# A vision tower on one core: the load queue waits for the token weights after tile 0's loads, the weights come in three parts, and one constant product goes

## The chip, the core and the metric

The kernel runs on one core of a Trainium2 chip. A core has TensorE (PE in the profile; PEld is its weight load), VectorE (DVE), ScalarE (ACT), GpSimd (POOL) and SyncE (SP), which here issues all DMAs. Each engine works through its own instructions in their order and waits on semaphores for the others. The metric is the device time of one launch in microseconds, as the median of several runs.

## The reference

The input is 32 images of 3 x 96 x 96 in fp32. Each is cut into 36 patches of 16 x 16 x 3 = 768 values, 1152 tokens in all. A token layer, an attention layer over channels and a layer of soft experts follow. The part that the change touches is the first:

```python
p = x.reshape(B, C, h, PATCH, w, PATCH).transpose(0, 2, 4, 3, 5, 1)
p = p.reshape(B, h * w, PATCH * PATCH * C)
p = _layernorm(p, ln1_g, ln1_b)               # over the 768 values
y = jnp.einsum('bnd,de->bne', p, W_proj)      # 768 -> 192
return _layernorm(y, ln2_g, ln2_b)
```

After it, h = layernorm(h + attention(h)), where queries, keys and values are products of h with 192 x 576 weights, and h = layernorm(h + experts(h)) with 8 experts of 4 slots each. All of it is fp32.

## The kernel before

The 1152 tokens are nine tiles of 128 for the token layer, and eleven groups of three images (108 tokens) for the rest. The first norm isn't applied to x. Its gain, its mean and its offset are folded into the weights: TensorE sums the weights' columns with the gain over 768 (`column_means`, L459, six products of 128 x 192, into `csp`), VectorE makes `wc = wt * gain - csp` in six pieces (`token_weights`, L713), TensorE makes the offset row (`offset`, L468, six products), and VectorE copies it (`token_offset`, L718). Then `token(t)` multiplies the turned tile xT with wc (L480, six products), and `token_out` (L740) scales the result by 1 / sigma of the token, which comes from the statistics of the plain tile xs (`x_stats`, L726, on VectorE; the power on GpSimd, L1211). So every tile is loaded twice, turned (`load_turned`, L375) and plain (`load_x`, L380), 384 KB each. The second norm follows, and `turn_h` (L491) turns h for the QKV products (L506 to L515).

An fp32 product is one MATMUL in the code and two passes, two entries, in the trace.

All engines' orders are written out by hand as lists of calls (L435 for the load queue, L680 for TensorE, L983 for VectorE). On TensorE the list starts with `first_products`: six products of a constant tile `still`, whose result nobody reads, right after VectorE has set that tile. Then come the column means, the offset, `token(0)`, `token(1)`, `token(2)`, and `turn_h(0)`.

SyncE's list starts with the first norm's gain and offset (gb), the token weights wt in two parts of three 128-row chunks each (288 KB a part, semaphores `wtok_in[0]` and `wtok_in[1]`), and tile 0's two loads. The identity, tile 1's two loads, tile 2's turned load, the small loads of the second norm, tile 3's turned load, tile 2's plain one, the three QKV weights and further tiles follow. The plain tiles have four buffers, so from tile 4 on `load_x(t)` waits until the statistics of tile t - 4 are done. The column means wait for the part of wt that holds their chunk, the offset for all parts.

Of the kernel before, what the change touches and what calls it, by code (L numbers as in the profile page):

```python
# [32 lines left out]
D = 192  # L33
HEADS, DH = 8, D // 8
PD = CH * PATCH * PATCH
KC = PD // 128
GI = 3
NG = (B + GI - 1) // GI
NT = NTOK // 128
# [7 lines left out]
NEG = -1.0e30  # L47
NQN = 2 * GI
NN = NQN + 2 * GI * DH
EPS_TOK, EPS_LN, EPS_L2 = 1e-6, 1e-5, 1e-6  # L50


def images(g):
    return min(GI, B - g * GI)


def tokens(g):
    return images(g) * TOK


def pieces(g):

    a, e, out = g * GI * TOK, g * GI * TOK + tokens(g), []
    while a < e:
        n = min(e, (a // 128 + 1) * 128) - a
        out.append((a // 128, a % 128, a - g * GI * TOK, n))
        a += n
    return out


def last_tile(g):
    return pieces(g)[-1][0]


def build(nc, x, x_t, w_tok, ln1_gb, ln2_g, ln2_b, g2col, b2col, w_qk, w_v, w_rest, w_proj, b_proj, temp, slots, scale,
# [3 lines left out]
    with ctx:  # L79
        def sb(name, shape):  # L80
            return ctx.enter_context(nc.sbuf_tensor(name, shape, F32))

        def sem(name):
            return ctx.enter_context(nc.semaphore(name))
# [4 lines left out]
        negmask = sb("negmask", [128, GI * SL])  # L89
        gb1 = sb("gb1", [128, 2, KC])  # L90
        gs1 = sb("gs1", [128, KC])
        wt = sb("wt", [128, KC, D])
        wc = sb("wc", [128, KC, D])
        bw = sb("bw", [128, D])
# [33 lines left out]
        y1 = sb("y1", [128, NB, D])  # L128
        xT = sb("xT", [128, KC * NTOK])
        st2 = sb("st2", [128, 2, 6])  # L130
# [60 lines left out]
        def csp():  # L191
            return ps[:, 0, 0:D]

        def bwp():
            return ps[:, 1, 0:D]
# [61 lines left out]
        h0_in = [sem(f"h0_in{g}") for g in range(NG)]  # L257
        ident_in = sem("ident_in")
        ln1_in = sem("ln1_in")
        wtok_in = [sem(f"wtok_in{i}") for i in range(2)]  # L260
        ln2_in = sem("ln2_in")
        wqkv_in = sem("wqkv_in")
        rows_in = sem("rows_in")
# [99 lines left out]
        @block.sync  # L363
        def _(sp):
            def load_norm1():
                sp.dma_start(gb1[:, :, :].rearrange("p t k -> p (t k)"), ln1_gb).then_inc(ln1_in, 16)

            def load_token_weights(i):
                k0 = i * KC // 2
                sp.dma_start(wt[:, k0:k0 + KC // 2, :].rearrange("p k e -> p (k e)"),  # L370
                             w_tok[:, k0 * D:(k0 + KC // 2) * D]).then_inc(wtok_in[i], 16)

            def load_turned(t):
                o = t * 128 * KC
                sp.dma_start(xT[:, o:o + KC * 128], x_t[:, o:o + KC * 128]).then_inc(xT_in[t], 16)  # L375

            def load_x(t):
                if t >= NB:
                    sp.wait_ge(st1_ready, t - NB + 1)
                sp.dma_start(xs[:, t % NB, :], x[t * 128:t * 128 + 128, :]).then_inc(x_in[t], 16)  # L380

            def load_ident():
                sp.dma_start(ident[:, :], ident_h).then_inc(ident_in, 16)

            def load_norm2():
                sp.dma_start(g2[:, :], g2col).then_inc(ln2_in, 16)
                sp.dma_start(b2[:, :], b2col).then_inc(ln2_in, 16)

            def load_imgsel():
                sp.dma_start(imgsel[:, :], imgsel_h).then_inc(imgsel_in, 16)  # L390

            def load_qkv():
                sp.dma_start(wqk[:, :], w_qk).then_inc(wqkv_in, 16)
                sp.dma_start(wv[:, :, :].rearrange("p m c -> p (m c)"), w_v).then_inc(wqkv_in, 16)
                sp.dma_start(wrest[:, :], w_rest).then_inc(wqkv_in, 16)

            def load_attention():
                sp.dma_start(tempc[:, :], temp).then_inc(attn_in, 16)
                sp.dma_start(wp[:, :, :], w_proj).then_inc(attn_in, 16)

            def load_rows():
                sp.dma_start(g2row[:, :], ln2_g.partition_broadcast(128)).then_inc(rows_in, 16)
                sp.dma_start(b2row[:, :], ln2_b.partition_broadcast(128)).then_inc(rows_in, 16)
                sp.dma_start(bprow[:, :], b_proj.partition_broadcast(128)).then_inc(rows_in, 16)

            def load_slots():
                sp.dma_start(negmask[:, :], negmask_h).then_inc(negmask_in, 16)
                sp.dma_start(spraw[:, :, :, :].rearrange("p f n q -> p f (n q)"),
                             slots.rearrange("(f p) n q -> p f (n q)", f=2)).then_inc(slots_in, 16)
                sp.dma_start(scl[:, :], scale.broadcast_to([F, 1])).then_inc(slots_in, 16)  # L410

            def load_experts():
                sp.dma_start(wd[:, :, :, :].rearrange("p f n h -> p f (n h)"), w_down).then_inc(experts_in, 16)
                sp.dma_start(bd[:, :], b_down).then_inc(experts_in, 16)
                sp.dma_start(own[:, :], own_h).then_inc(experts_in, 16)
                sp.dma_start(bu[:, :], b_up).then_inc(experts_in, 16)
                sp.wait_ge(cleared, 6)
                for j in range(4):
                    sp.dma_start(wu[32 * j:32 * j + HID, :, :], w_up[j]).then_inc(experts_in, 16)

            def regroup(g):
                sp.wait_ge(r_ready, last_tile(g) + 1)
                for t, p, q, n in pieces(g):
                    sp.dma_start(z[q:q + n, g, :], h0[p:p + n, t, 0:D]).then_inc(h0_in[g], 16)

            def store(g):
                if g < NG - 1:
                    sp.wait_ge(o4_ready, g + 1)
                else:
                    sp.wait_ge(o4_last, 1)  # L430
                ov = out.rearrange("b n d -> (b n) d")
                sp.dma_start(ov[g * GI * TOK:g * GI * TOK + tokens(g), :],
                             o4[0:tokens(g), g % NQ, :]).then_inc(out_done[g % NQ], 16)

            load_norm1(); load_token_weights(0); load_token_weights(1); load_turned(0); load_x(0)  # L435
            load_ident(); load_turned(1); load_x(1); load_turned(2); load_norm2(); load_turned(3)
            load_x(2); load_qkv(); load_turned(4); load_imgsel(); load_x(3); load_x(4); load_turned(5)
            load_turned(6); load_x(5); load_rows(); load_attention(); load_x(6); load_slots(); load_x(7)
            load_turned(7); load_x(8); load_turned(8); regroup(0); regroup(1); regroup(2); regroup(3)
            regroup(4); regroup(5); regroup(6); regroup(7); regroup(8); regroup(9); load_experts()  # L440
            regroup(10); store(0); store(1); store(2); store(3); store(4); store(5); store(6); store(7)
            store(8); store(9); store(10)
            for i in range(NQ):
                sp.wait_ge(out_done[i], 16 * len(range(i, NG, NQ)))

# [2 lines left out]
        def _(pe):  # L448
            def first_products():
                pe.wait_ge(still_ready, 1)  # L450
                for _ in range(6):
                    pe.matmul(ps[:, 2, 0:D], still[:, 0:128], still[:, :], start=True, stop=True)

            def column_means():
                pe.wait_ge(gs1_ready, 1)
                for kc in range(KC):
                    if kc % (KC // 2) == 0:
                        pe.wait_ge(wtok_in[kc // (KC // 2)], 16)
                    mm = pe.matmul(csp(), gs1[:, kc:kc + 1].broadcast_to([128, 128]), wt[:, kc, :],  # L459
                                   start=kc == 0, stop=kc == KC - 1)  # L460
                mm.then_inc(csp_ready, 1)

            def offset():
                pe.wait_ge(ln1_in, 16)
                pe.wait_ge(wtok_in[0], 16)
                pe.wait_ge(wtok_in[1], 16)
                for kc in range(KC):
                    mm = pe.matmul(bwp(), gb1[:, 1, kc:kc + 1].broadcast_to([128, 128]), wt[:, kc, :],  # L468
                                   start=kc == 0, stop=kc == KC - 1)
                mm.then_inc(bwp_ready, 1)  # L470
# [881 lines left out]
```

## Time and profile before

| | us |
|---|---|
| median of 3 runs | 112.63 (112.24 to 112.75) |
| the profiled execution | 112.18 |
| its span in the trace | 110.4 |
| TensorE busy with matmuls in the span | 101.7 |
| VectorE, ScalarE, GpSimd busy | 87.7, 67.5, 53.4 |

The span runs from the first instruction to the last. Times in the trace count from its start; what the profiled execution took beyond it lies before and after. A busy TensorE isn't TensorE at its peak, as matmuls are pipelined. A DMA's time "to landing" is counted from the start of its issue to the semaphore's last increment, and an issue of SyncE takes time itself.

### The profile page before, as it was taken

How to read it: one execution, taken by the hardware profiler on the slowest of the kernel's cores; microseconds unless marked ns; L12 is line 12 of the kernel's file. 1: busy time of each engine (PE TensorE's matmuls, PEld its weight loads, DVE VectorE, ACT ScalarE, POOL GpSimd, SP SyncE). 2: the span in 40 equal slices, each digit the busy share in tenths (PEclk: the TensorE clock that was granted, in tenths of full speed). 3: DMA queues.
4: the chain of work that ended last, by engine and by line, in shares of the span. 5: the costliest groups of instructions: out<-in, count | busy, mean ns of one | idle time of the engine just before them, and what ended most of it. 6: DMA issues, size and time to landing. Idle time of an engine off the chain costs nothing. (4 is left out here: it accounts for less than half of the span.)

```text
span 110.4 us, 4479 instructions
## 1 busy us (share of the span) xinstructions
PE 101.7 (92%) x1607; PEld 88.2 (80%) x1607; DVE 87.7 (79%) x380; ACT 67.5 (61%) x222; POOL 53.4 (48%) x126
## 2 busy tenths in 40 slices
PE   6999999999999999999999999799989989999900
PEld 6999989979999887887898887679779668879500
DVE  2129756968998958958977989999999897999960
ACT  4000023729563887798887996787785994476570
POOL 8800552263999887847204417906030340076880
PEclk9999999999999999999999999999999999999996
DMA  2999999469501111111000000010042000002232
GB/s 23 334 339 394 389 386 398 153 212 342 235 0 30 36 32 40 29 35 32 6 3 6 0 6 0 6 48 24 30 105 72 7 0 3 0 6 84 66 112 58
DMA packets 8554, 11.27 MB, mean 102 GB/s; under 512 B 2358, under 2 KB 5878, under 8 KB 8534
## 3 DMA queue, kind: packets, MB, share of 16 engines
q1 hardware_dynamic: 8533, 11.00, 29.5%
q8 instruction: 13, 0.21, 0.8%
q14 instruction: 8, 0.06, 0.2%
HBM read 9.22 MB, written 0.88 MB: 92 GB/s over the span
## 5 line engine op out<-in xcount | busy, mean ns | idle before, releaser
L480 PE MATMUL ps<-wc,xT 128*128 128x192 f32 x108 | 19.1, 330 | 0.0
L480 PEld LDWEIGHTS ps<-wc,xT 128*128 128x128 f32 x108 | 17.4, 190 | 0.7 <-issue 0.6
L1046 ACT ACTIVATE hT<-ps,b,g 128x128 f32<-128x128 f32 x18 | 7.3, 463 | 16.4 <-PE ps L491 16.3
L1068 ACT ACTIVATE km<-ps,imgsel 108x192 f32<-108x192 f32 (+1 forms) x32 | 11.1, 420 | 3.7 <-PE ps L515 3.6
L1256 POOL TENSOR_SCALAR mv<-mv 108x1 f32<-108x1 f32 (+1 forms) x11 | 3.0, 270 | 14.4 <-DVE mv L856 14.4
L568 PE MATMUL ps<-wp,yT 128*108 128x192 f32 (+1 forms) x44 | 9.3, 333 | 0.0
L664 PE MATMUL ps<-wu,hb 128*96 128x192 f32 (+1 forms) x44 | 9.2, 332 | 0.1
L1261 POOL TENSOR_TENSOR r<-mv,halves 108x2 f32<-108x2 f32 (+1 forms) x11 | 8.8, 803 | 0.8
L508 PE MATMUL ps<-wqk,hT 128*108 128x192 f32 (+1 forms) x44 | 9.0, 326 | 0.0
L726 DVE BATCH_NORM_STATS2 st<-xs 128x6 f32<-128x384 f32 x18 | 8.9, 537 | 0.0
L1249 POOL TENSOR_TENSOR rqt<-rn,tempc 128x6 f32<-128x6 f32 x11 | 2.2, 199 | 12.1 <-ACT rn L1105 12.1
L1207 POOL TENSOR_SCALAR var<-mv 128x1 f32<-128x1 f32 x9 | 2.0, 219 | 11.8 <-DVE mv L731 11.5
L1078 ACT ACTIVATE sqk<-km 108x576 f32<-108x576 f32 (+1 forms) x11 | 7.5, 683 | 0.0
L664 PEld LDWEIGHTS ps<-wu,hb 128*96 128x96 f32 (+1 forms) x44 | 6.5, 161 | 0.8 <-issue 0.4
L593 PE MATMUL ps<-sp,xnT 96*108 96x96 f32 (+1 forms) x44 | 6.2, 264 | 0.7 <-ACT xnT L1111 0.4
L568 PEld LDWEIGHTS ps<-wp,yT 128*108 128x108 f32 (+1 forms) x44 | 6.4, 170 | 0.5 <-DVE yT L836 0.2
L559 PE MATMUL ps<-vT,pc 32*32 32x37 f32 x512 | 6.8, 195 | 0.0
L1162 ACT ACTIVATE o<-z,sh,rstd 108x192 f32<-108x192 f32 x10 | 5.1, 543 | 2.8 <-DVE sh L980 2.8
L1269 POOL TENSOR_TENSOR rstd<-var,mhalf 108x1 f32<-108x1 f32 (+1 forms) x11 | 6.3, 576 | 0.9
L506 PE MATMUL ps<-hT,wv 128*128 128x108 f32 (+1 forms) x44 | 6.6, 273 | 0.0
L559 PEld LDWEIGHTS ps<-vT,pc 32*32 32x32 f32 x512 | 5.5, 104 | 1.3
L508 PEld LDWEIGHTS ps<-wqk,hT 128*108 128x108 f32 (+1 forms) x44 | 6.4, 171 | 0.0
(118 smaller groups left out, 296.6 us busy)
## 6 DMA issues: line engine op xcount, KB each, us to landing
xT<-in_x_t SPq DMA_DIRECT2D x9, 384.0 KB, 6.4
xs<-in_x SPq DMA_DIRECT2D x9, 384.0 KB, 6.2
out<-o SPq DMA_DIRECT2D x10, 81.0 KB
wt<-in_w_tok SPq DMA_DIRECT2D x2, 288.0 KB, 3.2
wqk<-in_w_qk SPq DMA_DIRECT2D x1, 192.0 KB, 5.9
wp<-in_w_proj SPq DMA_DIRECT2D x1, 192.0 KB, 10.0
wd<-in_w_down SPq DMA_DIRECT2D x1, 192.0 KB
z<-h SPq DMA_DIRECT2D x2, 81.0 KB
```

What stands on the lines that cost most here:

```text
L480: mm = pe.matmul(tokp(t), xT[:, o + kc * 128:o + (kc + 1) * 128], wc[:, kc, :], start=kc == 0, stop=kc == KC - 1)
L506: pe.matmul(vp(g)[:, m, :], wv[:, m, :], main, start=True, stop=False)
L508: pe.matmul(qkp(g)[:, m, :], main, wqk[:, m * D:(m + 1) * D], start=False, stop=False)
L559: mm = pe.matmul(yp(g)[r, m, i, :], pc[r, g % 2, GI * m + i, :], vT[r, m, g * GI + i, :], start=True, stop=True, tile_position=(32 * j, 32 ...
L568: mm = pe.matmul(prp(g), yT[:, g % NY, m, 0:images(g), :].rearrange("p i n -> p (i n)"), wp[:, m, :], start=m == 0, stop=m == 1)
L664: mm = pe.matmul(ytp(g), hb[:, e, i0:i0 + ni, :, :].rearrange("p i n q -> p (i n q)"), wu[:, e, :], start=e == 0, stop=e == 1)
L726: ins = dve.bn_stats(st1[:, t % 2, h, :], xs[:, t % NB, h * (PD // 2):(h + 1) * (PD // 2)])
L1046: ins = act.activation(hT[:, f, t * 128:(t + 1) * 128], htp(t)[:, f, :], ACT.Identity, bias=b2[:, f:f + 1], scale=g2[:, f:f + 1])
L1068: act.activation(km[0:n, g % NK, i, :], qkp(g)[:, 1, :], ACT.Copy, scale=imgsel[0:n, i:i + 1])
L1078: act.activation(sqk[0:n, g % 2, 0:ni, :], km[0:n, g % NK, 0:ni, :], ACT.Square).then_inc(sqk_ready, 1)
L1261: pool.tensor_tensor(r3[0:n, g, :], mv3[0:n, g, 1:3], halves[0:n, :], ALU.pow).then_inc(r3_ready, 1)
L1269: pool.tensor_tensor(rstd4[0:n, g:g + 1], var4[0:n, g:g + 1], mhalf[0:n, 0:1], ALU.pow).then_inc(rstd4_ready, 1)
```

## The change

The token weights come in three parts of two chunks, 192 KB each, with a semaphore for each. Behind the first tile's two loads SyncE waits until the last part has landed, and then issues the identity and the rest in the same order as before. Of the constant products five are left. The waits of the column means and of the offset follow the number of parts.

The load queue's first rows before (gb is the first norm's gain and offset, wt the token weights, xT and xs the turned and the plain tile, ident the identity, g and b the second norm's columns; one "x2" row stands for two issues):

```order
1 L366 DMA gb<-in_ln_gb 128x12
2 L370 DMA wt<-in_w_tok 128x576 x2
3 L375 DMA xT<-in_x_t 128x768
4 L380 DMA xs<-in_x 128x768
5 L383 DMA ident<-const_ident 128x128
6 L375 DMA xT<-in_x_t 128x768
7 L380 DMA xs<-in_x 128x768
8 L375 DMA xT<-in_x_t 128x768
```

And with the change:

```order
1 L367 DMA gb<-in_ln_gb 128x12
2 L371 DMA wt<-in_w_tok 128x384 x3
3 L376 DMA xT<-in_x_t 128x768
4 L381 DMA xs<-in_x 128x768
5 L387 DMA ident<-const_ident 128x128 [waits wtok_in2]
6 L376 DMA xT<-in_x_t 128x768
7 L381 DMA xs<-in_x 128x768
8 L376 DMA xT<-in_x_t 128x768
```

A third issue of wt stands ahead of tile 0's loads, and the identity's issue has a wait for the last part, wtok_in2; behind it the order is the same.

TensorE's first rows before (still is the constant tile, gs the gain over 768):

```order
1 L452 MATMUL ps<-still 128x192 [waits still_ready]
2 L452 MATMUL ps<-still 128x192 x5
3 L459 MATMUL ps<-wt,gs 128x192 [waits wtok_in0,gs1_ready]
4 L459 MATMUL ps<-wt,gs 128x192 x2
5 L459 MATMUL ps<-wt,gs 128x192 [waits wtok_in1]
6 L459 MATMUL ps<-wt,gs 128x192 x2
7 L468 MATMUL ps<-wt,gb 128x192 [waits wtok_in1,wtok_in0,ln1_in]
8 L468 MATMUL ps<-wt,gb 128x192 x5
```

And with the change:

```order
1 L457 MATMUL ps<-still 128x192 [waits still_ready]
2 L457 MATMUL ps<-still 128x192 x4
3 L464 MATMUL ps<-wt,gs 128x192 [waits wtok_in0,gs1_ready]
4 L464 MATMUL ps<-wt,gs 128x192
5 L464 MATMUL ps<-wt,gs 128x192 [waits wtok_in1]
6 L464 MATMUL ps<-wt,gs 128x192
7 L464 MATMUL ps<-wt,gs 128x192 [waits wtok_in2]
8 L464 MATMUL ps<-wt,gs 128x192
9 L473 MATMUL ps<-wt,gb 128x192 [waits wtok_in1,wtok_in2,wtok_in0,ln1_in]
10 L473 MATMUL ps<-wt,gb 128x192 x5
```

One product of the constant tile is gone, and the column means have three waits where they had two. The rest of TensorE's rows are as they were.

The diff, without the part of SyncE's list that is only set in other lines:

```diff
+WP = 3
...
-        wtok_in = [sem(f"wtok_in{i}") for i in range(2)]
+        wtok_in = [sem(f"wtok_in{i}") for i in range(WP)]
...
             def load_token_weights(i):
-                k0 = i * KC // 2
-                sp.dma_start(wt[:, k0:k0 + KC // 2, :].rearrange("p k e -> p (k e)"),
-                             w_tok[:, k0 * D:(k0 + KC // 2) * D]).then_inc(wtok_in[i], 16)
+                k0 = i * KC // WP
+                sp.dma_start(wt[:, k0:k0 + KC // WP, :].rearrange("p k e -> p (k e)"),
+                             w_tok[:, k0 * D:(k0 + KC // WP) * D]).then_inc(wtok_in[i], 16)
...
+            def weights_landed():
+                sp.wait_ge(wtok_in[WP - 1], 16)
...
-            load_norm1(); load_token_weights(0); load_token_weights(1); load_turned(0); load_x(0)
-            load_ident(); load_turned(1); load_x(1); load_turned(2); load_norm2(); load_turned(3)
...
+            load_norm1(); load_token_weights(0); load_token_weights(1); load_token_weights(2)
+            load_turned(0); load_x(0); weights_landed(); load_ident(); load_turned(1); load_x(1)
+            load_turned(2); load_norm2(); load_turned(3); load_x(2); load_qkv(); load_turned(4)
...
             def first_products():
                 pe.wait_ge(still_ready, 1)
-                for _ in range(6):
+                for _ in range(5):
                     pe.matmul(ps[:, 2, 0:D], still[:, 0:128], still[:, :], start=True, stop=True)
...
-                    if kc % (KC // 2) == 0:
-                        pe.wait_ge(wtok_in[kc // (KC // 2)], 16)
+                    if kc % (KC // WP) == 0:
+                        pe.wait_ge(wtok_in[kc // (KC // WP)], 16)
...
             def offset():
                 pe.wait_ge(ln1_in, 16)
-                pe.wait_ge(wtok_in[0], 16)
-                pe.wait_ge(wtok_in[1], 16)
+                for i in range(WP):
+                    pe.wait_ge(wtok_in[i], 16)
```

## Rows read from the trace of the kernel before

**Rows 1.** The page: share of the span, and 40 slices, in tenths

```profile
PE 101.7 (92%) x1607; PEld 88.2 (80%) x1607; DVE 87.7 (79%) x380; ACT 67.5 (61%) x222; POOL 53.4 (48%) x126
...
PE   6999999999999999999999999799989989999900
...
DVE  2129756968998958958977989999999897999960
```

**Rows 2.** Timeline of PE, 0 to 20 us: start, duration, engine, line, what

```profile
1.10 4.21 PE L452 MATMUL ps<-still 128*128 128x192 f32 x12 [1.10 <-DVE still L704]
5.10 2.54 PE L459 MATMUL ps<-wt,gs 128*128 128x192 f32 x12
7.48 2.11 PE L468 MATMUL ps<-wt,gb 128*128 128x192 f32 x12
9.43 6.01 PE L480 MATMUL ps<-wc,xT 128*128 128x192 f32 x36
```

**Rows 3.** Timeline of the weight loads (PEld), 0 to 20 us

```profile
4.78 2.56 PEld L459 LDWEIGHTS ps<-wt,gs 128*128 128x128 f32 x12
...
15.45 0.20 PEld L491 LDWEIGHTS ps<-ident,h 128*128 128x128 f32 x2 [0.30 <-DVE h L757]
```

**Rows 4.** Timeline of the load queue (SPq), 0 to 20 us

```profile
0.72 0.41 SPq L366 DMA_DIRECT2D gb<-in_ln_gb  x1
1.19 0.88 SPq L370 DMA_DIRECT2D wt<-in_w_tok  x2
...
2.59 0.43 SPq L380 DMA_DIRECT2D xs<-in_x  x1
3.06 0.43 SPq L383 DMA_DIRECT2D ident<-const_ident  x1
...
4.01 0.43 SPq L380 DMA_DIRECT2D xs<-in_x  x1
...
14.41 0.43 SPq L399 DMA_DIRECT2D wp<-in_w_proj  x1
18.04 0.33 SPq L380 DMA_DIRECT2D xs<-in_x  x1
```

**Rows 5.** Tile wt, its issue at 1.19 alone: time to landing

```profile
DMA to landing us min/median/max: 3.1/3.1/3.1
```

**Rows 6.** Tile wt, both of its issues: time to landing

```profile
DMA to landing us min/median/max: 3.1/3.2/3.4
```

**Rows 7.** Line L459, its weight loads: shortest, median and longest in ns

```profile
L459 PEld LDWEIGHTS ps<-wt,gs x12: 190/190/337, 4.8 to 7.2; 128*128 128x128 f32 x12
```

**Rows 8.** Windows: stretch, us, PE, PEld, DVE, ACT, POOL, clock, DMA, GB/s

```profile
2.00:7.00 5.00, 5.00 (x21) 5.00 (x20) 0.78 (x1) 0.00 (x0) 3.02 (x4) 1.00 0.89 287
5.00:6.00 1.00, 1.00 (x4) 1.00 (x4) 0.00 (x0) 0.00 (x0) 0.02 (x1) 1.00 0.80 227
6.00:7.00 1.00, 1.00 (x8) 1.00 (x8) 0.00 (x0) 0.00 (x0) 0.00 (x0) 1.00 0.93 352
7.00:12.00 5.00, 5.00 (x32) 5.00 (x32) 4.28 (x12) 0.00 (x0) 0.59 (x2) 1.00 1.03 390
```

**Rows 9.** Timeline of DVE, 0 to 20 us

```profile
7.68 2.04 DVE L713 SCALAR_TENSOR_TENSOR wc<-wt,gb,ps 128x192 f32<-128x192 f32 x6 [4.51 <-PE ps L459]
...
11.07 0.96 DVE L726 BATCH_NORM_STATS2 st<-xs 128x6 f32<-128x384 f32 x2
12.29 0.42 DVE L740 SCALAR_TENSOR_TENSOR y<-ps,rstd,bw 128x192 f32<-128x192 f32 x1 [0.26 <-issue]
...
13.90 0.42 DVE L740 SCALAR_TENSOR_TENSOR y<-ps,rstd,bw 128x192 f32<-128x192 f32 x1 [0.57 <-POOL rstd L1211]
```

**Rows 10.** Tile xs, its issue at 2.59: time to landing

```profile
DMA to landing us min/median/max: 5.1/5.1/5.1
```

**Rows 11.** Tile gb, its issue at 0.72: time to landing

```profile
DMA to landing us min/median/max: 1.6/1.6/1.6
```

**Rows 12.** Tile xs, its issue at 4.01: time to landing

```profile
DMA to landing us min/median/max: 5.8/5.8/5.8
```

More of the change, by code:

```diff
@@ L433, in store @@
                              o4[0:tokens(g), g % NQ, :]).then_inc(out_done[g % NQ], 16)
-            load_norm1(); load_token_weights(0); load_token_weights(1); load_turned(0); load_x(0)
-            load_ident(); load_turned(1); load_x(1); load_turned(2); load_norm2(); load_turned(3)
[L437 to L442, printed above, removed]
+            load_norm1(); load_token_weights(0); load_token_weights(1); load_token_weights(2)
+            load_turned(0); load_x(0); weights_landed(); load_ident(); load_turned(1); load_x(1)
+            load_turned(2); load_norm2(); load_turned(3); load_x(2); load_qkv(); load_turned(4)
+            load_imgsel(); load_x(3); load_x(4); load_turned(5); load_turned(6); load_x(5); load_rows()
+            load_attention(); load_x(6); load_slots(); load_x(7); load_turned(7); load_x(8)
+            load_turned(8); regroup(0); regroup(1); regroup(2); regroup(3); regroup(4); regroup(5)
+            regroup(6); regroup(7); regroup(8); regroup(9); load_experts(); regroup(10); store(0)
+            store(1); store(2); store(3); store(4); store(5); store(6); store(7); store(8); store(9)
+            store(10)
             for i in range(NQ):
```

## The prediction

> **What bounds the kernel now.** I read the page first, then the timeline of TensorE and of the load queue over the first 20 us, then the landings. TensorE's matmul row is busy 92% of the span, and its slices read 9 from the second slice to the 28th; only from there on do the 8s and 7s of TensorE stand beside a VectorE that is full [rows 1]. So until about 70 us the program is as long as TensorE's work, and something that TensorE does less at the start moves the rest forward. After 70 us VectorE and TensorE take turns; both get their inputs from the same stream, so they start as much earlier as it does.
>
> At the start TensorE runs without a gap through three blocks: the constant products (L452), the column means (L459), the offset (L468), and then tile 0's products (L480) [rows 2]. Each fp32 product stands as two passes, so 6 products are 12 entries. The constant products fill the time until the token weights are there: the column means' first weight load is at 4.78, with no wait named before it [rows 3]. Is that end set by the weights or by the products? The first part of the weights was issued at 1.19 [rows 4] and landed 3.1 later, at 4.29 [rows 5]; the second was issued some 0.46 later, after a 0.41 us issue, and by the larger of the two times, 3.4, it landed near 5.05 [rows 6]. At 4.78 part 0 had been there for half a microsecond. The products bound it, not the weights. That is the room that the change uses.
>
> TensorE has two rates here. The constant passes start 0.32 us apart ((4.78 - 1.10) / 12 is 0.31, with the very first one shorter), the offset's twelve (9.43 - 7.48) / 12 = 0.1625 apart [rows 2, 3]. The weight loads of the column means go from 337 down to 190 ns within the block [rows 7]. The granted clock reads 1.00 all through, with 4 weight loads from 5 to 6 us and 8 from 6 to 7 [rows 8], so the page's clock doesn't show this step; by the factor of two it is the lower of its two levels, 1.2 GHz, and then 2.4. How many column passes are slow? 12 passes take 7.48 - 5.10 = 2.38 [rows 2]; with a slow ones 0.32 a + 0.1625 (12 - a) = 2.38, so a = 2.7, and the rise falls near 5.10 + 2.7 x 0.32 = 5.97.
>
> **The change, part by part.**
>
> *One constant product less.* Two entries of 0.32 go from ahead of the column means. Their first weight load could then be at 4.78 - 0.64 = 4.14, their first matmul at 4.46. But the gain isn't 0.64. If the rise stays at 5.97, the means have 4.7 slow passes and not 2.7: 4.7 x 0.32 + 7.3 x 0.1625 = 2.69, so they end at 7.15 and not at 7.48. The gain is 0.33 us, two passes at the fast rate: up to the rise TensorE makes the same number of passes either way, only two more of them are useful. VectorE's weight scaling starts on the last column mean, at 7.68 [rows 9], so it, the offset and tile 0 move with it. I take -0.33. Bounds: 0 if TensorE is held by something else, -0.64 if the rise also came earlier.
>
> Of this the Trainium skill ("TensorE: Matmul & The Clock Gate", Part 1, on the clock gate) says that the warm-up is an amount of time and not a number of matmuls. By that rule the saving is the 0.33, by a count of products on real data it would be the 0.64; the one trace has no second start to decide between them.
>
> *Weights in three parts.* A third issue costs the queue one more of its 0.43 to 0.47 us [rows 4], so tile 0's two loads are issued 0.47 later, xs0 at 3.06 and not 2.59. What they need is not the issue but the transfers ahead of them, so their landing hardly moves: tile 0's statistics read xs0, landed at 2.59 + 5.1 = 7.7 [rows 10], on VectorE only after the six scalings that start at 7.68, some 2 us. Part 0 shrinks from 288 to 192 KB. The two old parts landed 0.76 apart, 288 KB each, so the missing 96 KB are 0.25: part 0 at 4.04, part 1 at 4.55, part 2 near 5.05. Needed: part 0 at 4.14, part 1 for the fifth pass at 4.46 + 4 x 0.32 = 5.7, part 2 for the ninth at about 6.5. Only the first is close: 0.1 us. If part 0 lands no earlier than the old part did, 4.29, TensorE loses 0.15, half of it given back because the rise doesn't move; landing earlier than 4.04 wins nothing. So -0.33 with an uncertainty of +0.15.
>
> *The hold of the load queue.* The identity's load now waits for part 2's landing, near 5.05, and was issued at 3.06. Everything queued behind goes with it: tile 1's two loads, tile 2, both columns of the second norm, tile 3, the three QKV loads, and so on, each 2.0 us later. Where does that end? At tile 6's x load, which waits for tile 2's statistics: the last issue before it ended at 14.41 + 0.43 = 14.84, and it came at 18.04 [rows 4], so 3.2 us of waiting take up the 2.0, and even the 0.33 by which 18.04 comes earlier.
>
> Issued later isn't landed later. The DMA engines moved 287 GB/s x 5 us = 1435 kB from 2 to 7 us [rows 8]; gb, the weights, xT0 and xs0 are 1382 kB. So the engines are on them until about 6.9, though they were all issued by 3.0; xs0's landing at 7.7 puts the tail of a transfer at about 0.7. The small norm load, issued at 0.72, landed 1.6 later [rows 4, 11], so from issue to the first bytes is about 0.9 at most. The identity issued at 5.1 has its bytes at hand at 6.0, tile 1's xT at 6.5: both before the engines run dry at 6.9. From 7 on they move 390 GB/s [rows 8], a 384 KB tile per 1.0 us, while the queue issues one per 0.47: the backlog builds up again. I count 0 to 0.3 us of later landing, not 2.0. The one load that has to be looked at is tile 1's x: it landed at 4.01 + 5.8 = 9.8 and VectorE takes it at 11.07, 10.74 after the shift [rows 4, 9, 12]. It has 0.9 us to spare, so 0. The other side: does the hold help? Only if transfers behind the weights slowed them. They start behind them on the same queue, and parts 0 and 1 were 0.76 apart at 288 KB, 388 GB/s, as fast as the engines go in the loaded stretch. I take 0, with bounds of -0.1 and, if all loads did land 2 us later, +0.85 (below).
>
> Here the Trainium skill ("DMA: Bandwidth & Descriptors", rules for kernel authors, and the anatomy of one DMA) speaks against the change: issue early and wait late, as a transfer has a fixed cost of about 2 us, most of it its completion. By that rule the hold leaves the engines idle for the completion and the next start; by the rows that time is filled by 786 kB of tile 0 that is already queued.
>
> **Sum.** -0.33 + 0 + 0. The profiled execution took 112.18 us, span 110.4 and 1.8 around it; it would come to 111.85. It lies 0.45 under the median of the three runs, 112.63, against which I predict: 112.63 - 0.33 = 112.3 us. A measurement of this kernel can tell about 0.5% from no change, 0.56 us: 112.07 to 113.19 is "the same".
>
> **Rivals.**
>
> *The rate rises later (slower).* Should part 0 land after 4.14, TensorE stands idle while still at the slow rate, where before it never had a gap. If the gap puts off the rise, each microsecond of it costs 1 - 0.1625 / 0.32 = 0.49. The gain of 0.33 is gone at 0.7 later, half a percent is lost at 1.8 later. At worst all 24 passes up to tile 0 are slow: 4.46 + 24 x 0.32 = 12.14 in place of 9.43, +2.7 us, 115.3; midway about 114. For it: only 0.1 us of cover. Against: a gap would be 0.15 at most by the old landing. Chance 0.09. The Trainium skill ("TensorE: Matmul & The Clock Gate", Part 1) has the chip watch activity in windows that run on their own, by which a short gap in the wrong place would do just this, and by which the instant of the rise also varies from run to run.
>
> *The loads really come 2 us late (worse, to the edge of slower).* Then tile 1's x lands at 11.85 and not by 10.74: statistics 1.1 late. Token output 0 has some 0.26 of idle before it at 12.29 [rows 9], so it and output 1 at 13.90 (behind its own statistics) come 0.85 later, and the turn of h of tile 0, for which TensorE already waits 0.3 [rows 3], as much. 0.85 - 0.33 = +0.5: 113.15. It decides from the point where landing is over 0.9 late. For it: the slump at 5 to 6 us, 227 GB/s [rows 8], shows that the engines can run short with loads queued. Against: the byte count above. Chance 0.13.
>
> *Nothing moves.* The hold holds back nothing that was in the weights' way, TensorE starts on part 0 about where it did, or a later wait eats the third of a microsecond. 112.6. Chance 0.14.
>
> *The whole product is saved.* If the rise comes with the real products instead of at its own instant, 0.64 go: 112.0. Chance 0.14.
>
> **Chances and range.** Forecast 0.50, with its own range 112.05 to 112.6; the rivals 0.09, 0.13, 0.14 and 0.14. Faster: 0.13 of the last and 0.07 of the forecast's scatter (the three runs differ by 0.5): 0.20. Slower: 0.09, half of the late loads' 0.13 and 0.02 of scatter: 0.17. The same: 0.63. Range 111.7 to 113.3: it leaves out the slower clock cases and a little below.
>
> **What would show it.** Right: 10 constant entries and column means from 4.1 to 4.2 with no gap, more of them slow than before, the offset ending 0.33 earlier; the identity's issue near 5.1; DMA slices without a hole at 6 to 7 us; statistics of tile 1 with no wait for a DMA; the same shift still there at 70 us. Wrong: a gap on TensorE ahead of the means, or slow loads in the offset block; a wait for xs on VectorE near 11; a shift near 0.64.

## The result, and the profile after

The changed kernel takes 113.03 us (median of 6 runs, 112.93 to 113.64) against 112.04 us for the kernel before in the same comparison: a ratio of 1.0098, interval 1.0058 to 1.0137. It is slower by about 1%. I had forecast 112.3 us, a third of a microsecond faster. A second comparison (the last experiment) gave 1.0061, interval 1.0027 to 1.0094. Executions over 1.5% above the fastest of their kernel are left out of the ratios: one of the 12 of "hold and five products with two parts", and one each of 35 and of 28 of the kernel before.

The page looks the same in its shares; the slices of the two engines, beside [rows 1]:

```profile
PE 102.2 (92%) x1605; PEld 88.4 (79%) x1605; DVE 87.9 (79%) x380; ACT 67.3 (60%) x222; POOL 53.4 (48%) x126
...
PE   6999989999999999999999999889989989998900
...
DVE  2119666677998959958987989999999897999960
```

TensorE, timeline of the first 20 us (start, duration, engine, line; lines are now 5 higher), beside [rows 2]:

```profile
1.10 3.57 PE L457 MATMUL ps<-still 128*128 128x192 f32 x10 [1.10 <-DVE still L709]
4.47 3.47 PE L464 MATMUL ps<-wt,gs 128*128 128x192 f32 x12
7.77 2.11 PE L473 MATMUL ps<-wt,gb 128*128 128x192 f32 x12
9.72 6.37 PE L485 MATMUL ps<-wc,xT 128*128 128x192 f32 x36
16.48 0.44 PE L496 MATMUL ps<-ident,h 128*128 128x128 f32 x2 [0.40 <-DVE h L762]
```

There are 10 constant passes, as meant, and the column means start at 4.47, where I had put 4.46. But they take 7.77 - 4.47 = 3.30 us and not 2.69, and the first turn of h, at 15.45 before, stands at 16.48 with a wait for VectorE. That is +1.03 us, and it is all of the loss in the profile: span less that start is 111.4 - 16.48 = 94.9 now and 110.4 - 15.45 = 94.9 before.

VectorE in the same stretch, beside [rows 9]:

```profile
7.97 2.04 DVE L718 SCALAR_TENSOR_TENSOR wc<-wt,gb,ps 128x192 f32<-128x192 f32 x6 [4.80 <-PE ps L464]
...
12.41 1.02 DVE L731 BATCH_NORM_STATS2 st<-xs 128x6 f32<-128x384 f32 x2 [0.97 <-DMA xs<-in_x]
...
14.93 0.42 DVE L745 SCALAR_TENSOR_TENSOR y<-ps,rstd,bw 128x192 f32<-128x192 f32 x1 [0.57 <-POOL rstd L1216]
```

Tile 1's statistics wait 0.97 us for their x. Before, they started at 11.07 with no wait. They hold up tile 0 as well, since VectorE's list has them ahead of tile 0's output, and tile 1's output ahead of the last step of h for tile 0. Why did x come so late? The load queue, beside [rows 4], and its one wait for the weights:

```profile
1.19 1.36 SPq L371 DMA_DIRECT2D wt<-in_w_tok  x3
...
3.06 0.43 SPq L381 DMA_DIRECT2D xs<-in_x  x1
6.38 0.33 SPq L387 DMA_DIRECT2D ident<-const_ident  x1
...
7.23 0.43 SPq L381 DMA_DIRECT2D xs<-in_x  x1
```

```profile
SPq L387 <- DMA wt<-in_w_tok: 2.9, 1, 2.9
```

The hold ended at 6.38, where I had written 5.05, so tile 1's x was issued at 7.23. The landings: part 0 alone, then all three parts, then tile 1's x from that issue (beside [rows 5, 6, 12]):

```profile
DMA to landing us min/median/max: 2.4/2.4/2.4
```

```profile
DMA to landing us min/median/max: 2.4/2.5/4.3
```

```profile
DMA to landing us min/median/max: 5.2/5.2/5.2
```

Part 0 was there at 1.19 + 2.4 = 3.6, earlier than my 4.04. The last part, issued at 2.11, took 4.3 and landed at 6.4. Tile 1's x landed at 7.23 + 5.2 = 12.4. What the DMA engines moved (last number, GB/s; the one before it is the busy share of the engines), beside [rows 8]:

```profile
2.00:7.00 5.00, 5.00 (x17) 5.00 (x16) 0.81 (x1) 0.00 (x1) 3.02 (x4) 1.00 0.85 226
4.00:5.00 1.00, 1.00 (x5) 1.00 (x4) 0.00 (x0) 0.00 (x0) 1.00 (x1) 1.00 0.96 171
5.00:6.00 1.00, 1.00 (x4) 1.00 (x4) 0.00 (x0) 0.00 (x0) 0.02 (x1) 1.00 0.91 180
7.00:12.00 5.00, 5.00 (x32) 5.00 (x32) 3.44 (x10) 0.00 (x0) 0.31 (x2) 1.00 0.95 313
```

The kernel before, from 4 to 5 us:

```profile
4.00:5.00 1.00, 1.00 (x5) 1.00 (x4) 0.00 (x0) 0.00 (x0) 1.00 (x1) 1.00 1.06 405
```

So the engines moved 171 GB/s there, where the kernel before had 405, and they were busy all the same (0.96 of their time): the single packet took longer. The packets of that microsecond, before and with the change:

```profile
DMA packets 163, 0.40 MB, mean 405 GB/s; under 512 B 16, under 2 KB 16, under 8 KB 163
```

```profile
DMA packets 100, 0.17 MB, mean 171 GB/s; under 512 B 13, under 2 KB 76, under 8 KB 100
```

The kernel before has a slow microsecond too, the next one: 227 GB/s from 5 to 6 [rows 8]. Behind the hold the changed kernel moved 313 GB/s in place of 390 from 7 to 12. From 2 to 12 us the engines moved 5 x (226 + 313) = 2695 kB, and before 5 x (287 + 390) = 3385 kB.

### The profile page after: what moved, and what is told of

Read it like the earlier page. It is cut to its first block and busy times, and to the rows that moved or that the text cites. A ratio compares the mean times of both kernels' runs of the same rounds, so it can differ in the third digit from the quotient of the medians.

```text
span 111.4 us, 4477 instructions
## 1 busy us (share of the span) xinstructions
PE 102.2 (92%) x1605; PEld 88.4 (79%) x1605; DVE 87.9 (79%) x380; ACT 67.3 (60%) x222; POOL 53.4 (48%) x126
## 5 line engine op out<-in xcount | busy, mean ns | idle before, releaser
L1254 POOL TENSOR_TENSOR rqt<-rn,tempc 128x6 f32<-128x6 f32 x11 | 2.2, 202 | 12.6 <-ACT rn L1110 12.1
```

## The experiments

Theory A said that the hold alone makes tile 1's x late; B, that the third part does, by slower transfers; C, that it is TensorE's slow rate, which rose later (8.6 slow column passes by the working of the prediction, 3.30 = 0.32 a + 0.1625 (12 - a), so at about 7.2 and not 5.97). Four kernels take the change apart. Ratios are those of the compared runs to the kernel before, with their 95% intervals. They differ from the quotient of the two medians by up to 0.2%. The kernel before had a median of 111.86 us beside the first four kernels, 112.18 beside the next four and 112.00 beside the last four, each group on a chip of its own. A trace shows one execution, and not always a typical one. Each diff shows only the lines that matter: the first three against the kernel before, with its two parts written as WP = 2, the version to beat both against the kernel of two and four chunks, and the others against the change.

**The hold alone** (two parts, six products):

```diff
-            load_turned(0); load_x(0); load_ident(); load_turned(1); load_x(1)
+            load_turned(0); load_x(0); weights_landed(); load_ident(); load_turned(1); load_x(1)
```

> The hold alone, with the weights in two parts and six constant products. Theory A (the hold makes tile 1's x late): the last weight part lands where before had it or later, 5.0 to 5.3, the identity is issued just behind it, tile 1's x lands 1.5 to 2.5 later than before's 9.8 and VectorE waits for it ahead of its statistics; +0.7 to +1.0 us against before. Theory B (the third part is what slows the transfers, the hold is harmless while they keep their pace): last part at 5.05, tile 1's x at 9.8 to 10.3, no wait, 0 to +0.2 us. Theory C (the fewer constant products and the later rise of TensorE's rate cost it): 0.

111.97 us, ratio 1.0002 (0.9971 to 1.0033). Neither theory as written: the time stayed, as B has it, but the mechanism that A names was there in the trace. The hold ended at 5.1, tile 1's x was issued at 6.00 and landed 5.7 later:

```profile
11.71 1.02 DVE L731 BATCH_NORM_STATS2 st<-xs 128x6 f32<-128x384 f32 x2 [1.16 <-DMA xs<-in_x]
```

```profile
4.92 2.11 PE L464 MATMUL ps<-wt,gs 128*128 128x192 f32 x12
...
15.78 0.44 PE L496 MATMUL ps<-ident,h 128*128 128x128 f32 x2 [0.40 <-DVE h L762]
```

The turn is only 0.33 later than in the profile of before. And this was one of the slower executions, 112.49 us with a median of 111.97. The fastest of the twelve took 111.37 us, 1.1 less, and no x as late as 11.7 fits into that (the section on the fourteen profiles has the constant). So with the hold alone the x isn't this late in every execution.

**Three parts alone** (no hold, six products):

```diff
-WP = 2
+WP = 3
...
-            load_norm1(); load_token_weights(0); load_token_weights(1)
+            load_norm1(); load_token_weights(0); load_token_weights(1); load_token_weights(2)
```

> Three parts alone, without the hold and with six constant products. Theory A: no wait for tile 1's x, 0 us within 0.2. Theory B: the last part lands near 6.4 as it did with the change, every load behind it is later than before, tile 1's x by 1 us or more, +0.3 to +1.0 us. Theory C: 0.

112.48 us, ratio 1.0039 (1.0006 to 1.0073). B holds in direction and place. The transfers, and VectorE's waits at tile 0 and at tile 1:

```profile
4.00:5.00 1.00, 1.00 (x5) 1.00 (x4) 0.00 (x0) 0.00 (x0) 1.00 (x1) 1.00 0.95 149
```

```profile
10.23 1.02 DVE L731 BATCH_NORM_STATS2 st<-xs 128x6 f32<-128x384 f32 x2 [0.76 <-DMA xs<-in_x]
...
12.37 1.02 DVE L731 BATCH_NORM_STATS2 st<-xs 128x6 f32<-128x384 f32 x2 [0.62 <-DMA xs<-in_x]
```

This profile is of the slowest of the twelve executions, 113.20 us.

**Five products alone:**

```diff
-                for _ in range(6):
+                for _ in range(5):
```

> Five constant products alone. By my prediction's term: column means from 4.15 unless part 0 (288 KB) lands later, then from about 4.35, and -0.2 to -0.33 us. Theory C: the rise of TensorE's rate comes near 7.2 as with the change and not near 6.0, column means end 0.3 later than before, +0.3 to +0.5 us. Theories A and B say nothing but that it isn't +1.

111.77 us, ratio 0.9986 (0.9957 to 1.0015). C had +0.3 to +0.5 us for this kernel, and that lies above the interval: fewer products don't cost the change its time. (Within one execution a late rise can still cost: here it came near 6.9, and this was the slowest of the twelve, 112.33 us.) My -0.33 us (-0.3%) lies in the interval, and so does zero. Part 0 of 288 KB landed at 4.4, so the weight loads had a gap ahead of the means:

```profile
4.51 2.99 PEld L464 LDWEIGHTS ps<-wt,gs 128*128 128x128 f32 x12 [0.35 <-issue]
```

**The change without its hold** (three parts, five products):

```diff
-            load_turned(0); load_x(0); weights_landed(); load_ident(); load_turned(1); load_x(1)
+            load_turned(0); load_x(0); load_ident(); load_turned(1); load_x(1)
```

> The change without its hold: three parts, five constant products. Theory A: the loss goes whole, at or below before: -0.3 to 0 us, and 0.7 to 1.3 us under the changed kernel. Theory B: the loss stays, +0.5 to +1. Theory C: a third of it stays, +0.3.

112.42 us, ratio 1.0037 (1.0004 to 1.0071): part of the loss seems to go with the hold and part to stay with the three parts, though this interval overlaps with both of the change's. The next four ask where each part acts.

**The hold behind tile 1's loads:**

```diff
-            load_turned(0); load_x(0); weights_landed(); load_ident(); load_turned(1); load_x(1)
+            load_turned(0); load_x(0); load_ident(); load_turned(1); load_x(1); weights_landed()
```

> The changed kernel with the hold moved behind tile 1's two loads; three parts, five products. Theory L (with the hold the lateness of tile 1's x is what sets the end; the rest of the loads behind the hold have room): about as the change without the hold, 0.4% over before, 0.6 us under the change. Theory M (any load behind the hold counts, such as tile 2's turned x or the QKV weights): as the change, 1.0% over before.

112.12 us, ratio 1.0001 (0.9975 to 1.0027). Theory L, and more, as it had left 0.4%: three loads moved out of the hold's reach, and the loss is gone, although all later loads are still held. Tile 1's x, and the turn:

```profile
11.18 1.02 DVE L731 BATCH_NORM_STATS2 st<-xs 128x6 f32<-128x384 f32 x2 [0.59 <-DMA xs<-in_x]
```

```profile
15.24 0.44 PE L496 MATMUL ps<-ident,h 128*128 128x128 f32 x2 [0.40 <-DVE h L762]
```

**Parts of two and four chunks**, no hold, five products:

```diff
+WB = (0, 2, 6)
+                k0, k1 = WB[i], WB[i + 1]
```

> No hold, five products, weights in two issues of two and four chunks: rows of 1536 and of 3072 bytes. Theory N (the number of issues ahead of tile 0's loads is what costs): no loss, part 0 near 3.7, no gap on TensorE, xs of tile 0 near 7.7, -0.1 to -0.4 us against before. Theory S (rows of 1536 bytes are what slows the transfers from 4 to 6 us): half of the loss, +0.1 to +0.3 us, and a last part after 5.4.

111.86 us, ratio 0.9973 (0.9941 to 1.0006). The small first part lands at 1.19 + 2.5 = 3.7, TensorE starts the means at 4.46 with no gap, and the transfers keep their pace, 341 GB/s from 4 to 5. As theory N has it, though the gain over before isn't clear of the measurement.

**Three parts, each in one piece in DRAM**, no hold, five products:

```diff
-                             w_tok[:, k0 * D:(k0 + KC // WP) * D]).then_inc(wtok_in[i], 16)
+                             w_tok[i]).then_inc(wtok_in[i], 16)
```

> No hold, five products, three parts, but each part lies in one piece in DRAM (its rows of 1536 bytes one behind the other instead of 4608 bytes apart). Theory K (the stride in DRAM is what slows the transfers, as every part touches all the rows' pages): last part near 5.1, the loss of 0.4% gone. Theories N and S: as the change without the hold, +0.4%, last part near 6.

112.21 us, ratio 0.9985 (0.9959 to 1.0011). Undecided by the time, which lies under the strided version's 1.0037 with intervals that overlap, on another chip. With the kernel that has the hold behind tile 1's loads, it is the second of three parts that lost nothing on this chip, so the 0.4% of the three parts stands on one chip only. The trace speaks against theory K: the transfers are as slow from 4 to 5, and the last part lands at 2.11 + 3.8 = 5.9.

```profile
4.00:5.00 1.00, 1.00 (x5) 1.00 (x4) 0.00 (x0) 0.00 (x0) 1.00 (x1) 1.00 0.85 135
```

**The hold and five products with two parts:**

```diff
-WP = 3
+WP = 2
```

> The change with its hold and five products, but two parts: the hold alone gave 0, the five products alone -0.1%. If the three parts are the half that the hold multiplies: within 0.2% of before, some 0.9 us under the change, tile 1's x late by 1 us and less on VectorE. If hold and fewer products together are what cost: over 0.5% slower.

112.22 us, ratio 0.9983 (0.9957 to 1.0009). The hold ended at 5.0, tile 1's x was issued at 5.82, and VectorE waited 1.32 us for it, more than expected, but to 11.88 only. So the hold costs the time only together with the third part.

**A third issue of 6 KB ahead of tile 0** (two parts, no hold, five products; the load goes into a tile that nobody reads):

```diff
+                sp.dma_start(spare[:, :], ln1_gb).then_inc(spare_in, 16)
```

> Two weight parts of 288 KB with 2304-byte rows, and a third issue of 6 KB (the first norm's columns again, into a tile that nobody reads) ahead of tile 0's loads; no hold, five products. Theory N (a third issue in the start is what slows the transfers): the microsecond from 4 to 5 moves under 220 GB/s as in all kernels with three parts, tile 1's statistics wait to 11.4 or later. Theory S (many short rows do): 4 to 5 moves 320 to 410 GB/s as with two parts, no wait.

111.99 us, ratio 1.001 (0.9978 to 1.0042), 254 GB/s from 4 to 5 us, 255 from 5 to 6. That is between the two expectations. There is no wait for tile 1's x, but this says little: the x landed at 11.2, and VectorE came to it only at 11.57, as the column means began late (last section). Nor is the rate a clean answer, since the extra load fell into that microsecond in small packets:

```profile
DMA packets 248, 0.25 MB, mean 254 GB/s; under 512 B 160, under 2 KB 160, under 8 KB 248
```

**All weights in one issue with rows of 1536 bytes** (no hold, five products):

```diff
+                sp.dma_start(wt[:, :, :].rearrange("p (a k) e -> p a (k e)", a=RP),
+                             w_tok.rearrange("a p c -> p a c"))
```

> All 576 KB of the weights in one issue, but cut into rows of 1536 bytes; no hold, five products, the column means wait for the whole. Theory S: 4 to 5 us moves under 220 GB/s, the landing comes near 6 (4.8 from its issue). Theory N: 4 to 5 moves 320 or more, landing near 4.8 to 5.0. TensorE has a gap behind the constants in both cases, so the time as such tells little: 0 to +0.7%.

114.14 us (4 runs, 113.86 to 114.21), ratio 1.0196 (1.0158 to 1.0234), far above my 0.7% at most. In this profile the row length alone doesn't slow the transfers; theory S falls:

```profile
4.00:5.00 1.00, 0.67 (x3) 0.17 (x1) 0.00 (x0) 0.00 (x0) 1.00 (x1) 1.00 1.07 395
```

The time has another cause. The whole landed at 5.3, the weight loads had a gap of 1.24 us, and afterwards all 12 column passes took (9.41 - 5.44) / 12 = 0.33 us, the slow rate:

```profile
5.44 4.18 PE L464 MATMUL ps<-wt,gs 128*128 128x192 f32 x12 [0.76 <-DMA wt<-in_w_tok]
9.41 2.17 PE L473 MATMUL ps<-wt,gb 128*128 128x192 f32 x12
```

This is what my first rival describes. It is the longest of such gaps. Four other kernels had shorter ones in their weight loads at the slow rate (0.35 us with five products alone, 0.19 with hold and two parts, 0.92 and 0.91 in the two kernels of the last section), and there the rate rose at 6.9, 5.4, 7.0 and 5.9, no later than in kernels without a gap. That the gap put off the rise to after 9.4 is therefore likely here and not shown.

**A version to beat both:** two and four chunks, five products, no hold, the identity behind tile 1's loads.

```diff
-            load_turned(0); load_x(0); load_ident(); load_turned(1); load_x(1)
+            load_turned(0); load_x(0); load_turned(1); load_x(1); load_ident()
```

> A version that should beat both: five products, weights in two and four chunks, no hold, and the identity's load behind tile 1's two, so that tile 1's x, which starts the chain to the end, comes 0.17 us (64 KB) earlier. If the start of tile 1's statistics sets the end (end = that start + 99 us in the waiting kernels): -0.3 to -0.6% against before, at or 0.1 us under the same without the swap. If the identity is missed at the first turn (near 14.7): no gain.

111.65 us, ratio 0.9981 (0.9956 to 1.0006). Well under the change on the same chip (1.0061, below), not clear of the kernel before. The swap of the identity bought nothing that could be measured. Its profile is also one of two in which the column means began only at 5.08, with the first part of the weights there since 3.7; the cause is told in the last section.

**The change once more:**

> The changed kernel once more, beside the others on one chip. Last weight part near 6.4 and 4 to 5 us under 220 GB/s again, the hold ending there; tile 1's statistics wait to 12.2 to 12.6 and the span is that start + 99.0; +0.7 to +1.3%. If the late last part was one execution's chance: hold ends near 5, +0.2%.

112.83 us, ratio 1.0061 (1.0027 to 1.0094). The late last part was no chance of one execution: 155 GB/s from 4 to 5, the hold to 5.93, tile 1's x issued at 6.77.

```profile
SPq L387 <- DMA wt<-in_w_tok: 2.4, 1, 2.4
```

```profile
12.63 1.02 DVE L731 BATCH_NORM_STATS2 st<-xs 128x6 f32<-128x384 f32 x2 [2.02 <-DMA xs<-in_x]
```

```profile
16.70 0.44 PE L496 MATMUL ps<-ident,h 128*128 128x128 f32 x2 [0.40 <-DVE h L762]
```

This was the slowest of its eleven executions. Here TensorE's rate had risen by about 5.1, two microseconds before the first profile's, the column means ended over a microsecond earlier (6.71 for 7.77), and the end came no earlier. With tile 1's x this late, what TensorE gains ahead of it is lost.

## One number that the fourteen profiles share

In each kernel the time from the first turn of h to the end of the span is the same, and where VectorE waited for tile 1's x, so is the time from those statistics to the turn:

| kernel | weight issues | GB/s, 4 to 5 us | tile 1's x issued | its statistics start (wait) | turn of h | span | span - turn |
|---|---|---|---|---|---|---|---|
| before | 2 | 405 | 4.01 | 11.07 (none) | 15.45 | 110.4 | 94.9 |
| the change | 3 | 171 | 7.23 | 12.41 (0.97) | 16.48 | 111.4 | 94.9 |
| the change again | 3 | 155 | 6.77 | 12.63 (2.02) | 16.70 | 111.6 | 94.9 |
| hold alone | 2 | 334 | 6.00 | 11.71 (1.16) | 15.78 | 110.7 | 94.9 |
| three parts alone | 3 | 149 | 4.48 | 12.37 (0.62) | 16.44 | 111.4 | 95.0 |
| five products alone | 2 | 331 | 4.01 | 11.23 (none) | 15.61 | 110.5 | 94.9 |
| no hold | 3 | 214 | 4.48 | 11.58 (0.63) | 15.65 | 110.6 | 94.9 |
| hold later | 3 | 146 | 4.48 | 11.18 (0.59) | 15.24 | 110.1 | 94.9 |
| two and four chunks | 2 | 341 | 4.00 | 10.45 (none) | 14.75 | 109.6 | 94.9 |
| in one piece | 3 | 135 | 4.48 | 11.41 (0.57) | 15.48 | 110.4 | 94.9 |
| hold, two parts | 2 | 328 | 5.82 | 11.88 (1.32) | 15.94 | 110.8 | 94.9 |
| third issue of 6 KB | 2 + 1 | 254 | 4.48 | 11.57 (none) | 15.93 | 110.8 | 94.9 |
| one issue, short rows | 1 | 395 | 3.76 | 13.04 (none) | 17.41 | 112.3 | 94.9 |
| identity later | 2 | 350 | 3.54 | 11.03 (none) | 15.39 | 110.2 | 94.8 |

Waiting kernels have turn - statistics = 4.06 or 4.07. Without a wait it is 4.3 to 4.4, as the power on GpSimd for tile 0 is then what output 0 waits for. So only one event of the start counts, and everything after it takes the same time to 0.2 us. Two things set that event: the landing of tile 1's x, and the end of the column means, which hangs on when they can begin and on when TensorE's rate rises. Tile 1's x landed at 9.6 to 10.7 us in the five kernels with one or two weight issues and no hold, at 11.2 to 12.4 with a third issue and no hold ahead of it, at 11.7 and 11.8 with two parts behind the hold, and at 12.4 and 12.6 with the change.

## Why the prediction was wrong

The measured 113.03 us lies inside my range, 111.7 to 113.3, but that is luck: I had counted it from 112.63, the median of three runs, and beside the change the kernel before took 112.04. The direction was wrong.

*The start of the column means, right.* 4.47 against 4.46 forecast, no gap, part 0 in time. Their end wasn't: 7.77 for 7.15, as the rate rose at 7.2 and not at 5.97, where I had left it. That isn't my first rival, whose late rise needs a gap ahead of it.

*What the constant product gives, not refuted and not shown.* Forecast -0.33; alone it measured 0.9986 with an interval of three tenths of a percent to each side. The instant of the rise, which moved by over 2 us between profiles, hides a term of this size, so whether 0.33 or 0.64 is right stays open. In the changed kernel it could give nothing, since the end waits for tile 1's x.

*The hold: the step that failed.* I wrote "I count 0 to 0.3 us of later landing, not 2.0" and "It has 0.9 us to spare, so 0". The landing was 2.6 us later (12.4 for 9.8). The step rested on two inputs. The first was part 2 near 5.05, worked out by splitting the bytes that two issues had moved. With three weight issues the transfers moved 135 to 214 GB/s from 4 to 5 us in all six such profiles, with two 328 to 405 in all six, with one 395, and the last part landed at 5.8 to 6.4, with the change at 6.4 and 5.9. Tile 1's x was issued 3.2 and 2.8 us later, not 2.0. The second was that the backlog of tile 0 covers the hold. From 7 to 12 us the held kernels (the change twice, the hold alone, the hold with two parts) moved 304 to 349 GB/s, all the others 357 to 392. So the hold does leave the engines short, with two parts as well: from 7 to 8 us their busy share was 0.78 and 0.85 there, and 1.05 in the profile of before (the share can read a little over 1). Tile 1's x came at 11.7 and 11.8 in these two profiles, and at 9.8 to 10.7 in the four with two parts and no hold.

A smaller step failed beside it, in the part on the three parts: of tile 0's loads I wrote "so their landing hardly moves". Tile 0's x landed at 9.1 with the change and not at 7.7, and with the three parts alone at 10.2, where VectorE waited for it.

One reading of the page was off, and nothing hangs on it: TensorE's slices read 9 from the second to the 25th and 7 in the 26th, not 9 up to the 28th.

On this the Trainium skill ("DMA: Bandwidth & Descriptors", rules for kernel authors, and the anatomy of one DMA) had it better than my byte count: the wait for a transfer belongs late, as only then is its fixed part covered, about 2 us of mostly completion. The trace agrees in direction with 313 GB/s for 390. The section on the anatomy is about transfers that GpSimd issues, and these are SyncE's; 2 us of idling as such no run shows.

*The rival that came true* was the second, "the loads really come 2 us late", to which I gave 0.13: its place (tile 1's x, then output 1, then the turn of h) and its rule were right, with a cost of 1.03 in the profile in place of 0.5, as the landing was 12.4 and not 11.85. I had put its threshold at 0.9 us of lateness, which the hold alone reached as well.

*Why the hold or the parts alone cost less.* With three parts and no hold the x is issued at 4.48 and the slow stretch makes it late by itself, 1.0039 on one chip and nothing on another. With the hold and two parts it is issued at 5.8 to 6.0. Why that costs nothing in the median is argued, not shown. A landing at 11.7 makes a span of 110.7, as 4.07 + 94.9 = 99.0 us lie between it and the end. The median spans with the hold were 110.2 (alone) and 110.3 (with five products), those of the kernel before beside them 110.1 and 110.4. So by estimate the x came earlier in most of these executions than in the two profiles, about when the kernel before got to it for the other reason, the column means' end. The change's 17 executions have spans from 110.5 to 111.8. Moving the hold behind tile 1's loads took the whole loss away, from 1.0098 and 1.0061 to 1.0001. That shows that the place is among the three loads in between; that it is tile 1's x, the waits and the 99.0 us show. VectorE's order, which puts tile 1's statistics ahead of tile 0's output, was changed in no run.

*What stays open.* Why three issues of weights slow the transfers at 4 to 6 us. By one profile each, it isn't the row length (one issue with the same rows ran at 395) and not the stride in DRAM (135 without it). These two kernels keep the weights in DRAM in the same way and differ in the number of issues, and with it in the order in which the rows are read, which speaks for one of the two. The 6 KB issue gave 254, between the two groups, but with 160 packets under 512 bytes where the kernel before had 16, so it doesn't settle it. Nor does the slow stretch belong to three issues alone: from 5 to 6 us the kernel before moved 227 GB/s and the one with five products 203. Over 2 to 7 us the groups still stand apart, 214 to 242 with three weight issues and 263 to 297 with two.

## What to carry to other kernels

A wait put into a load queue moves every load behind it, so look for the first of them that has a consumer early in the chain and put the wait behind that one. The landing time of a transfer that is split differently can't be worked out from bytes alone: with three weight issues the last part landed 0.7 to 1.3 us later than with two of equal size (5.8 to 6.4 for about 5.1). And where the profiles of several kernels are at hand, take the time from one event near the start to the end: if it is constant, as 94.9 us here, the changes are worth what they do to that event.

## What the runs showed of the hardware that I had not expected

TensorE's rate rose, by the same working in each profile, between 4.9 us or before (hold alone: all twelve column passes fast, 2.0 us for the block) and 7.2 us (the change), with no gap on TensorE in either and the granted clock at 1.00 throughout. From passes at 0.32 us and at 0.1625, two microseconds of later rise are worth one at the column means' end. The Trainium skill ("TensorE: Matmul & The Clock Gate", Part 1) says that the instant varies between runs, by half a microsecond to either side; here it does by over 2 us. It fits that the kernel before spreads from 111.3 to 112.8 us over 27 runs in the last comparison, while the change's runs lie within 0.7 (6 runs) and 1.2 (11 runs).

The column means also wait for `gs`, the gain over 768 (VectorE's `mean_shares`, 128 x 6). In twelve profiles that instruction takes 0.58 to 0.81 us and ends at 3.17 or 3.18, wherever it starts between 2.36 and 2.60. In the two others (identity later, third issue) it ends at 5.02. GpSimd's last memset starts at 3.17 and ends at about 5.0. VectorE and GpSimd of the kernel with the identity later:

```profile
2.36 2.66 DVE L714 TENSOR_SCALAR gs<-gb 128x6 f32<-128x6 f32 x1 [1.31 <-DMA gb<-in_ln_gb]
```

```profile
2.41 0.74 POOL L1206 MEMSET pr<- 128x768 f32 x1
...
3.17 1.83 POOL L1208 MEMSET hb<- 128x2048 f32 x1
```

So the small instruction seems to slip in where one memset ends, or to sit through the next, which is 1.83 us long here. The Trainium skill ("SBUF — State Buffer", who interferes with whom) calls the port pair that VectorE and GpSimd share an exclusive lock: whichever of some VectorE instructions, `tensor_scalar` among them, and GpSimd's issues first has it for its whole instruction, and the other one waits. The ends at 3.17 and 5.02 agree with that. With five constant products TensorE's weight loads were idle for 0.91 us by it; with six, whose last weight load ends at 4.8, it would be some 0.3 by estimate. No kernel with the memset elsewhere was run.
